# One exponential for four images, an image gated by ScalarE, sums over adjacent numbers, and stores on two queues

## What is computed

```python
x = x + conv_branch(group_norm(x))      # deformable 3x3 sampling, 8 groups of 4 channels, then @ w_out + b_out
t = to_tokens(x)                        # 8 images x 256 tokens x 32 channels
u = layer_norm(t)
t = t + softmax(u @ u.T) @ u            # attention, one 256 x 256 matrix of scores per image
v = layer_norm(t)
p = softmax(v @ router_w + router_b)    # 8 experts
top_p, top_i = top_k(p, 2); top_p /= top_p.sum()
t = t + sum_k top_p[k] * (v @ expert_w[top_i[k]] + expert_b[top_i[k]])
```

## Time and profile before

| | before |
|---|---|
| timed runs, us | 90.08, 90.57, 90.48; median 90.48 |
| the profiled execution: its own time, us | 90.25 |
| its span, first to last instruction, us | 88.5 |
| granted TensorE clock, mean (1.0 is 2.4 GHz) | 0.898 |
| busy TensorE / VectorE / GpSimd / ScalarE, us | 73.2 / 58.3 / 50.4 / 30.2 |

### The profile page before, as it was taken

One profiled execution on the slowest core, in us unless ns is written; L12 is line 12 of the kernel. 1 busy time (PEld: TensorE's weight loads), 2 busy tenths in 40 slices (PEclk: granted clock), 3 DMA queues, 4 the chain that ended last, 5 costly groups with the idle time before them and its releaser, 6 DMA issues.

```text
span 88.5 us, 1516 instructions
## 1 busy us (share of the span) xinstructions
PE 73.2 (83%) x569; PEld 61.1 (69%) x569; DVE 58.3 (66%) x108; ACT 30.2 (34%) x63; POOL 50.4 (57%) x82
## 2 busy tenths in 40 slices
PE   2999999899999998979999958967665799799500
PEld 2989598789999887969999937944124596265200
DVE  1156303609978999999899544871167689999710
ACT  0451103995693569200000020448945500010010
POOL 5109999983996999999981000077013300399800
PEclk9999999999999999999999999999999955555555
DMA  0412431048600000000000000000000000000014
GB/s 0 121 35 39 107 52 13 8 117 242 178 0 4 0 7 0 4 0 0 0 11 0 0 0 0 0 0 0 7 0 0 0 0 0 0 0 0 0 31 88
DMA packets 5256, 2.35 MB, mean 27 GB/s; under 512 B 4432, under 2 KB 4785, under 8 KB 5249
## 3 DMA queue, kind: packets, MB, share of 16 engines
q1 hardware_dynamic: 4817, 2.07, 9.9%
q10 hardware_dynamic: 432, 0.20, 0.8%
HBM read 0.81 MB, written 0.26 MB: 12 GB/s over the span
## 4 chain that ended last, share of the span: by engine, by line
DVE 27%; PE 18%; ACT 8%; POOL 7%; issue 4%; DVEq 0%
PE ps L618 10%; DVE prod L297 6%; POOL image_all L508 6%; DVE image_all L986 6%; ACT image_all L876 5%; PE ps L605 3%; DVE tok_v L1104 2%; DVE image_all L1196 1%; ACT tok_q L866 1%; PE ps L674 1%; PE ps L684 1%; PE ps L657 1%; POOL prod L509 1%; DVE tok_c L1099 1%; DVE tok_s L1098 1%
## 5 line engine op out<-in xcount | busy, mean ns | idle before, releaser
L517 PE MATMUL ps<-wide_ident 128*128 128x128 f32 x108 | 15.2, 296 | 1.8 <-POOL wide_ident L377 1.8
L517 PEld LDWEIGHTS ps<-wide_ident 128*128 128x128 f32 x108 | 13.8, 206 | 2.8 <-POOL wide_ident L377 1.8
L986 DVE TENSOR_TENSOR image_all<-ps,images 128x896 f32<-128x896 f32 (+4 forms) x8 | 13.2, 1689 | 0.4 <-PE ps L605 0.4
L618 PE MATMUL ps<-wide_ident,image_all 128*128 128x128 f32 (+2 forms) x100 | 11.7, 274 | 0.9 <-DVE image_all L986 0.9
L618 PEld LDWEIGHTS ps<-wide_ident,image_all 128*128 128x128 f32 (+2 forms) x100 | 10.9, 138 | 1.2 <-DVE image_all L986 1.2
L605 PE MATMUL ps<-wide_ident,prod 128*128 128x128 f32 x81 | 9.9, 275 | 0.2
L605 PEld LDWEIGHTS ps<-wide_ident,prod 128*128 128x128 f32 x81 | 8.8, 141 | 0.8 <-DVE prod L297 0.7
L293 POOL TENSOR_TENSOR my<-prob,hat 128x384 f32<-128x384 f32 x8 | 7.9, 1010 | 0.7 <-DVE ps L293 0.7
L494 POOL TENSOR_SCALAR tok_q<-tok_ln 128x256 f32<-128x256 f32 x2 | 1.7, 850 | 11.4 <-DVE tok_ln L1108 11.4
L297 POOL TENSOR_TENSOR prod<-my,hat 128x1152 f32<-128x1152 f32 x3 | 8.0, 2651 | 0.2
L297 DVE TENSOR_TENSOR prod<-ps,hat 128x1152 f32<-128x1152 f32 x6 | 7.9, 1350 | 0.1
(11 more groups left out here) (178 smaller groups left out, 128.6 us busy)
## 6 DMA issues: line engine op xcount, KB each, us to landing
images<-images SPq DMA_DIRECT2D x2, 300.0 KB, 4.1
images<-images SPq DMA_DIRECT2D x2, 280.0 KB, 3.6
x_tok<-in_x SPq DMA_DIRECT2D x4, 64.0 KB, 2.4
out_dram<-prod SPq DMA_DIRECT2D x3, 64.0 KB, 2.2
x_rows<-in_x SPq DMA_DIRECT2D x1, 128.0 KB, 2.7
x_rows<-in_x ACTq DMA_DIRECT2D x1, 128.0 KB, 3.3
expert<-in_expert_w SPq DMA_DIRECT2D x4, 32.0 KB
out_dram<-prod ACTq DMA_DIRECT2D x1, 64.0 KB, 2.5
```

What stands on the lines that cost most here:

```text
L517: pe.matmul(pbank(bank, P), ident, ident, start=True, stop=True)
L618: ins = pe.matmul(ps[0:last, SAMPLED, c * NJ:(c + 1) * NJ], taps[:, ty % SLOTS, tx, c, 0:last], ident, start=(ty == 0 and tx == 0 and c == 0),
L986: v.tensor_tensor(taps[:, ty % SLOTS, t0:t1, :, y0 * NI:y1 * NI], bcast(coef_rows(ty, t0, t1).rearrange("p (t j) -> p t j", j=P)[:, :, y0 ...
```

## The change

Line numbers of the kernel before are used throughout; the shapes stay the same where nothing is said.

```diff
-        CONV_OUT = PV = 3
-        SCORE = (3, 4, 5, 6, 7, 0, 2, 1)
-        EXPERT = (7, 5, 6, 1, 0, 2, 5, 6)
+        CONV_OUT, PV = 3, 4
+        SCORE = (4, 5, 6, 7, 0, 1, 2, 3)
+        SAMP_T = (7, 0, 1, 2)
+        EXPERT = (7, 6, 3, 1, 0, 2, 6, 3)
         GATE_T = 7
-        POOL_SUMS = ((0, 0, 2), (1, 0, 2), (1, 2, 3))
-        VECTOR_SUMS = ((0, 2, 4), (1, 3, 4))
+        ACT_GATED = 5
+        VECTOR_GATED = tuple(n for n in range(NI) if n != ACT_GATED)
+        POOL_SUMS = ((0, 0, 2), (1, 0, 2))
+        VECTOR_SUMS = ((0, 2, 4), (1, 2, 4))
...
+        def gated_by_channel(ga, q0, q1):
+            return gated[:, ga, q0:q1, :, :, :].rearrange("p q h e c -> p (q h) (e c)").rearrange("p t (c e) -> p t c e", e=NE)
...
             sp.wait_ge(result_ready, 1)
-            for side in range(2):
-                sp.dma_start(tokens_of(out, 0, side), on_chip(result, 0, side)).then_inc(stored, 16)
+            sp.dma_start(tokens_of(out, 0, 1), on_chip(result, 0, 1)).then_inc(stored, 16)
...
-                g.wait_ge(gated_ready, ga * GI + q1)
+                g.wait_ge(gated_ready, sum(n < ga * GI + q1 for n in VECTOR_GATED))
+                if ga * GI + q1 > ACT_GATED:
+                    g.wait_ge(act_gated, 1)
...
-            for half, bank in enumerate((SPARE, 0)):
-                pe.wait_ge(samp_ready, half + 1)
-                for b in range(2):
-                    ins = pe.transpose(...)
-                ins.then_inc(samp_T, 1)
+            for b in range(4):
+                pe.wait_ge(samp_ready, b + 1)
+                pe.transpose(pbank(SAMP_T[b], P), ...).then_inc(samp_T, 1)
...
-                for q in range(GI):
-                    for h in range(HALVES):
+                for h in range(HALVES):
+                    for q in range(GI):
                         ins = pe.matmul(pbank(SCORE[ga * GI + q], 2 * P, h * 2 * P), ...)
-                    ins.then_inc(scores_done, 1)
+                ins.then_inc(scores_done, 1)
...
-                pe.wait_ge(exp_done, (ga + 1) * GI)
+                pe.wait_ge(exp_done, ga + 1)
...
+            for b in (0, 2):
+                act.wait_ge(samp_T, b + 1)
+                act.activation(sampT[:, :, :, b].rearrange("p n y -> p y n"), ...)
...
-            def exp_scores(n):
+            def exp_scores(ga):
+                act.wait_ge(scores_done, ga + 1)
+                b = SCORE[ga * GI]
+                act.activation(probs[:, ga * GI:(ga + 1) * GI, :, :].rearrange("p n h s -> p (n h s)"),
+                               ps[:, b:b + GI, :].rearrange("p b j -> p (b j)"), ACT.Exp, bias=neg_bound[:, :]).then_inc(exp_done, 1)
...
+            def gate_experts(h):
+                q = ACT_GATED - GI
+                for e in range(NE):
+                    ins = act.activation(gated[:, 1, q, h, e, :], pbank(EXPERT[ACT_GATED], C, (h * NE + e) * C), ACT.Copy,
+                                         scale=gate_s[:, GT + h * GI + q, e:e + 1])
+                return ins
...
+            act.wait_ge(gate_s_ready, 1)
+            act.wait_ge(experts_done, ACT_GATED + 1)
+            gate_experts(0)
             keep_gateT()
+            gate_experts(1).then_inc(act_gated, 1)
...
+            act.wait_ge(result_ready, 1)
+            act.dma_start(tokens_of(out, 0, 0), on_chip(result, 0, 0)).then_inc(stored, 16)
             act.wait_ge(last_result_ready, 1)
             act.dma_start(tokens_of(out, 1, 1), on_chip(result, 1, 1)).then_inc(stored, 16)
...
+            for b in range(4):
+                j = slice(b * NJ // 4, (b + 1) * NJ // 4)
                 v.tensor_tensor(samp[:, j, :], sampled[:, j, :], bcast(rden[:, j], 2, GC), ALU.mult).then_inc(samp_ready, 1)
+            for b in (1, 3):
+                v.wait_ge(samp_T, b + 1)
+                v.tensor_copy(sampT[:, :, :, b].rearrange("p n y -> p y n"), ...).then_inc(sampT_copied, 1)
...
+                to = gated[:, ga, q, :, :, :]
+                if any(ga == a and q0 <= q < q1 for a, q0, q1 in VECTOR_SUMS):
+                    to = gated_by_channel(ga, q, q + 1).rearrange("p h c e -> p h e c")
...
+            for n in VECTOR_GATED:
+                gated_experts(n)
             for ga, q0, q1 in VECTOR_SUMS:
-                                      gated[:, ga, q0:q1, :, :, :].rearrange("p q h e c -> p (q h) c e"), AX, ALU.add)
+                                      gated_by_channel(ga, q0, q1), AX, ALU.add)
```

More of the change, by code:

```diff
@@ L643, in _ @@
             pe.wait_ge(x_proj_ready, 1)
-            for half, bank in enumerate((SPARE, 0)):
-                pe.wait_ge(samp_ready, half + 1)
-                for b in range(2):
-                    ins = pe.transpose(pbank(bank, P, b * P),
-                                       samp[:, (2 * half + b) * 4 * G:(2 * half + b + 1) * 4 * G, :].rearrange("p j c -> p (j c)"), ident)
-                ins.then_inc(samp_T, 1)
+            for b in range(4):
+                pe.wait_ge(samp_ready, b + 1)
+                pe.transpose(pbank(SAMP_T[b], P), samp[:, b * 4 * G:(b + 1) * 4 * G, :].rearrange("p j c -> p (j c)"),
+                             ident).then_inc(samp_T, 1)
             pe.wait_ge(late_ready, 1)
-            pe.wait_ge(sampT_ready, 1)
-            pe.wait_ge(sampT_copied, 1)
+            pe.wait_ge(sampT_ready, 2)
+            pe.wait_ge(sampT_copied, 2)
             for ga in range(GA):
@@ L856, in _ @@
             keep_rows(5)
[L858 to L861, removed]
+            for b in (0, 2):
+                act.wait_ge(samp_T, b + 1)
+                act.activation(sampT[:, :, :, b].rearrange("p n y -> p y n"),
+                               pbank(SAMP_T[b], P).rearrange("p (y n) -> p y n", n=NI), ACT.Copy).then_inc(sampT_ready, 1)
             def squares(ga, centred, squared):
@@ L871, in deviation @@
                 inv_sqrt(tok_r[:, g], tok_d[:, g], tok_v[:, g], eps[:, 0:1], 1.0 / C).then_inc(ready, 1)
-            def exp_scores(n):
-                act.wait_ge(scores_done, n + 1)
-                act.activation(probs[:, n, :, :].rearrange("p h s -> p (h s)"), pbank(SCORE[n]), ACT.Exp,
-                               bias=neg_bound[:, :]).then_inc(exp_done, 1)
+            def exp_scores(ga):
[3 more added lines that the diff above has]
+                               ps[:, b:b + GI, :].rearrange("p b j -> p (b j)"), ACT.Exp, bias=neg_bound[:, :]).then_inc(exp_done, 1)
             def keep_attT():
@@ L895, in _ @@
                 deviation(ga, tok_summed, ga + 1, tok_rstd_ready)
-            for n in range(NI):
-                exp_scores(n)
+            for ga in range(GA):
+                exp_scores(ga)
             keep_attT()
@@ L1085, in _ @@
             v.wait_ge(rden_ready, 1)
-            for half in range(2):
-                j = slice(half * NJ // 2, (half + 1) * NJ // 2)
+            for b in range(4):
+                j = slice(b * NJ // 4, (b + 1) * NJ // 4)
                 v.tensor_tensor(samp[:, j, :], sampled[:, j, :], bcast(rden[:, j], 2, GC), ALU.mult).then_inc(samp_ready, 1)
-            v.wait_ge(samp_T, 2)
-            v.tensor_copy(sampT[:, :, :, 2:4].rearrange("p n y b -> p b y n"),
-                          pbank(0, 2 * P).rearrange("p (b y n) -> p b y n", b=2, n=NI)).then_inc(sampT_copied, 1)
+            for b in (1, 3):
+                v.wait_ge(samp_T, b + 1)
+                v.tensor_copy(sampT[:, :, :, b].rearrange("p n y -> p y n"),
+                              pbank(SAMP_T[b], P).rearrange("p (y n) -> p y n", n=NI)).then_inc(sampT_copied, 1)
             def group(ga):
@@ L1188, in choose, with gated_experts @@
                 v.wait_ge(chosen, 1)
-                then(v.tensor_tensor(gate_s[:, :, :], second[:, :, :], bcast(scaled, 2, NE), ALU.mult))
-            def gated_experts(ga):
+                v.tensor_tensor(gate_s[:, :, :], second[:, :, :], bcast(scaled, 2, NE), ALU.mult).then_inc(gate_s_ready, 1)
+                v.wait_ge(gate_s_ready, 1)
+            def gated_experts(n):
+                ga, q = n // GI, n % GI
                 by_image = gate_s[:, group(ga), :].rearrange("p (h q) e -> p q h e", h=HALVES)
-                for q in range(GI):
-                    n = ga * GI + q
-                    v.wait_ge(experts_done, n + 1)
-                    v.tensor_tensor(gated[:, ga, q, :, :, :], pbank(EXPERT[n]).rearrange("p (h e c) -> p h e c", h=HALVES, e=NE),
-                                    bcast(by_image[:, q, :, :], 3, C), ALU.mult).then_inc(gated_ready, 1)
+                to = gated[:, ga, q, :, :, :]
+                if any(ga == a and q0 <= q < q1 for a, q0, q1 in VECTOR_SUMS):
+                    to = gated_by_channel(ga, q, q + 1).rearrange("p h c e -> p h e c")
+                v.wait_ge(experts_done, n + 1)
+                v.tensor_tensor(to, pbank(EXPERT[n]).rearrange("p (h e c) -> p h e c", h=HALVES, e=NE),
+                                bcast(by_image[:, q, :, :], 3, C), ALU.mult).then_inc(gated_ready, 1)
             v.wait_ge(pv_done, 1)
```

12 lines of the change are left out of this document (5 added, 7 removed).

## The result

| | before | changed |
|---|---|---|
| median, us | 90.48 | 89.63 |
| all runs, us | 90.08 to 91.12 (5) | 89.41 to 91.07 (5) |
| ratio to before | | 0.988, 95% interval 0.9836 to 0.9925 |
| profiled execution: time / span, us | 90.25 / 88.5 | 91.07 / 89.0 |
| time outside the span, us | 1.75 | 2.07 |

The ratios in this document compare only executions within 1.5% of the fastest of their kernel, so they can differ from the quotient of the medians; here that leaves out 91.07 and 90.98. The mean of all five changed executions is 90.13, that of the five before 90.48.

What follows compares the result with a forecast made beforehand. No engine was taken as the bound in the last third, but a chain hopping between engines. Gains of 0.14 + 0.43 + 0.3 = 0.87 us off the median 90.48 gave 89.6 us, range 88.6 to 90.5.

Steps and rivals of the forecast that it cites:

- Quarters: Sampled values: products, transposes and copies in quarters instead of halves; gain 0.14 us, bounds 0 and 0.3.
- One exponential: Attention: one long exponential per group instead of four; gain 0.43 us, bounds 0 and 0.66.
- VectorE's row: End: one product fewer, four scattered products dearer, two reductions cheaper; stores may start 0.13 us later.
- ScalarE's image: End: one image gated by sixteen small ScalarE products, 0.32 us each, hidden by VectorE's second reduction; cost nothing.
- Stores: End: two stores issued from each of two queues; 0.3 us earlier after taking off 0.13, bounds 0 and 0.6.
- second rival: VectorE's products at the end: scattered writes cost nothing, stores start earlier; 88.8 us, chance 0.14.
- fourth: VectorE's reductions at the end: adjacent numbers reduce no faster, 1.89 us each; 90.9 us, chance 0.06.
- rival 5: TensorE's clock falls before the attention's weighting, adding some 1.5 to 3 us on the chain; 91.9 us, chance 0.04.

Runs made afterwards that it cites:

- halves: Changed kernel with the sampled values in halves again instead of quarters; 89.73 us in one execution.
- stores as before: Changed kernel with three stores on SyncE's queue and one on ScalarE's again; median 91.16 us, ratio 1.0032 to the kernel before.
- merged exponentials alone: Kernel before with only the merged exponentials and the banks and matmul order they need; median 89.87 us, ratio 0.9889 to the kernel before.
- repeated measurement: Changed kernel measured again without any edit, six executions; median 90.93 us, ratio 0.9989 to the kernel before.
- early reduction with idle matmuls: Changed kernel with group 0's reduction moved ahead and 8 idle matmuls in TensorE's gaps; median 89.05 us, ratio 0.9795 to the kernel before.
- eight exponentials: Changed kernel with one exponential per image again; 90.72 to 92.57 us in four executions, ratio 1.0024 to the kernel before.
- all on VectorE: Changed kernel with image 5 gated by VectorE again instead of ScalarE; 90.58 us in one execution.
- plain sums: Changed kernel with products written and read in the order h, e, c for all images, as before; 89.67 to 94.83 us, ratio 0.9971.
- early reduction: Changed kernel with group 0's reduction ahead of images 6 and 7's products, its TensorE sum ahead of group 1's bias; median 89.76 us, ratio 0.9872.

## Why the prediction was right

The median was met to 0.03 us and the range held it. The terms inside the span came out, each from the run that isolates it; the median itself was partly luck (below).

- **Quarters**, 0.14 forecast: 0.20 (halves: 2.03 against 1.83), inside the span.
- **One exponential**, 0.43: 0.42 alone on the kernel before, 0.48 on the changed one. A long one takes 1.97, forecast 1.96.
- **VectorE's row**, 5.71 for the products and 2.36 for the reductions: 5.68 and 2.35. A scattered product takes 1.085 where I took 1.04; neighbours overlap by a little more than I allowed. The first store comes 8.72 behind B; forecast 84.55 - 75.84 = 8.71. ScalarE's image stayed hidden, with products of 0.29 that follow each other every 0.19. Taking it back costs 0.6.
- **Stores**, 0.3 net and 0.43 gross: from B to the end 12.66 before and 12.43 now, 0.23 net; 0.45 gross (stores as before).

At equal clock the gain from A to the end of the span is 0.20 + 0.42 + 0.23 = 0.85; forecast 0.87. The second rival (scattering is free) and the fourth (adjacent numbers reduce no faster) are refuted by 1085 ns and by 1214 against 1900 ns. The Trainium skill's penalty for each access to a new line (SBUF — State Buffer, Specifications (TRN2)) agrees with both figures. What the Trainium skill says of issuing from several engines (DMA: Bandwidth & Descriptors, Issuing engines are not separate DMA queues) names the right saving, but it is not small here: 0.45 us gained, where one issue takes 0.72.

**What the sum took for nothing: the time outside the span.** The forecast subtracted 0.87 from the whole time, as if the 1.75 us outside the span stayed. They did not. In all 40 executions of the kernel before with a recorded span they are 1.69 to 1.82, in the merged exponentials alone 1.68 to 1.77, in the halves 1.73. In all 62 executions of kernels with the quarters they are 2.03 to 2.23. So some 0.35 us of the 0.85 is lost again, and it goes with the quarters, which gain only 0.20; the halves rest on one execution, and what in the quarters costs it is open. That leaves about 0.5, and fastest against fastest shows 0.67 in the result (90.08, 89.41) and 0.53 in the repeated measurement (90.10, 89.57). That the medians differ by 0.85 as well, 90.48 and 89.63, is partly luck: the median of before lies 0.40 above that kernel's fastest, the changed one's only 0.22.

**What the sum left out** is rival 5, which I gave 0.04, in a smaller form. The clock did fall earlier, not ahead of the attention but ahead of the second router product, in 2 of the 5 executions of the result (mean clock 0.888 and 0.889, 91.07 and 90.98 us) and in 3 of the next 6. Had a third of the five had it, the median of the result would have been near 91, outside the range. The median of the repeated measurement, 90.93, is outside. I argued that the change closes a gap of TensorE and opens none. It does close the one at 62.63, but the next one grows, since TensorE is done sooner with the weighting of group 1 while what it then waits for hangs on group 0. Before, and in the changed kernel:

```profile
66.36 0.44 PE L666 MATMUL ps<-wide_ident,tok_c 128*128 128x128 f32 x2 [0.35 <-DVE tok_c L1148]
```

```profile
66.59 0.44 PE L672 MATMUL ps<-wide_ident,tok_c 128*128 128x128 f32 x2 [0.62 <-DVE tok_c L1170]
```

The sparse stretch behind it (in the repeated measurement TensorE is busy for 0.29 of the us from 68 to 69) also begins earlier after A. The price is 24.25 - 23.74 = 0.5 us from A to B: L672 takes 0.70 instead of 0.44 and L705 1.07 instead of 0.63, and 0.2 of that is covered, since VectorE's next step waited that long for ScalarE before. Where it happens the gain of the exponentials is gone. These executions also reached A late, which is a second loss: in the early reduction with idle matmuls, where the clock never falls early, spans are still 86.6 or 87.3 to 87.6.

That idle matmuls in the gaps put the fall off is shown: with them it came 23 us and more after A in all four kernels' profiles, and in none of their 30 executions was the mean clock under 0.925. Why the change has the early fall and the kernel before has not is only half told apart. Of the runs with both the merged exponential and the quarters, some executions of each kernel that was timed in rounds have it; without the one (eight exponentials, 4 executions) or the other (merged alone, 6), and in the kernel before, none that I could identify. That the two together shift the sparse stretch far enough, by 0.6 us, fits; no run tried another shift.

A rival that no run separates from this is the late start. In the profiles with both edits and no idle matmuls, the clock fell 16.4 to 16.8 us after A where A came at 51.90 to 52.39, but 19.3 after it at an A of 51.66 (all on VectorE) and 18.8 after it at 56.85 (plain sums). In the repeated measurement the mean clock is 0.886 at spans of 88.7 to 88.9, and 0.898 to 0.900 at 87.5 as well as at 89.7 and 90.2. The kernel before, without any edit, has 0.894 to 0.897 at spans of 88.4 and up to 0.926 at 89.3 to 89.5. So where the clock falls depends on when the kernel reaches A too. A late start alone is not enough, as the eight exponentials with A at 52.00 show. But the six executions of merged alone hardly reached such starts: by their spans, less the 36.64 from A to the end, A was at 51.3 to 51.9, an estimate. The repeated measurement (0.9989, 0.9918 to 1.006) shows how much hangs on it.

## What to carry to other kernels

When several parallel pieces feed a queue of stores, put each group's reduction as early as its inputs allow: the early reduction was worth 0.85 us, as much as the whole change gained inside the span. Count a layout change on both sides: scattering four products for two gathered reductions came out even. Compare the time outside the span as well as the span: here a finer hand-over gained 0.20 inside and went with 0.35 lost outside. After every shortening of a chain, look at the granted clock behind it; work that moves by half a microsecond can leave a sparse stretch where the clock then falls, and a few idle matmuls, counted by their true length and put only into gaps, keep it up.

## What the runs showed of the hardware

A start that the clock row doesn't show: in the head of the kernel, which the change doesn't touch, the same idle matmuls took, before and in the changed kernel's profile,

```profile
5.35 1.47 PE L517 MATMUL ps<-wide_ident 128*128 128x128 f32 x10
```

```profile
5.43 2.36 PE L525 MATMUL ps<-wide_ident 128*128 128x128 f32 x10
```

and A came at 51.48 and 52.32. In the profile of the plain sums the head lost 5 us in this way, and the convolution's 24 records took 5.57 us instead of 3.82. The granted clock is told as 1.0 in all of them. So equal matmuls ran at two paces under one row of the clock, and before its first change that row alone doesn't tell how fast TensorE runs; that the slower pace is the clock is likely but not shown.

VectorE reads 128 bytes apart and writes 32 bytes apart at nearly the same price: 1.7 ns per number (1884 ns for 1024) and 1.8 (1085 ns for 512) instead of 1.02, with 0.16 us taken off as fixed. An activation may read four banks of PSUM in one go: 2048 numbers in 1.97 us, where four of 512 took 2.4.
